# Four-layer graph network on one core: three of ScalarE's instructions in another place of its order

## Time and profile before

| | us |
|---|---|
| median of 3 runs | 5209.99 (5206.79 to 5223.11) |
| the profiled execution, its own time | 5213.31 |
| its span in the profile | 5211.5 |

### The profile page before, as it was taken

One profiled execution on the slowest core, in us unless ns is written; L12 is line 12 of the kernel. 1 busy time (PEld: TensorE's weight loads), 2 busy tenths in 40 slices (PEclk: granted clock), 3 DMA queues, 4 the chain that ended last, 5 costly groups with the idle time before them and its releaser, 6 DMA issues. The chain is left out here.

```text
span 5211.5 us, 74853 instructions
## 1 busy us (share of the span) xinstructions
PE 4348.2 (83%) x20185; PEld 3268.9 (63%) x20185; DVE 4031.9 (77%) x13139; ACT 2978.4 (57%) x7633; POOL 3114.9 (60%) x2813
## 2 busy tenths in 40 slices
PE   3999999999948888857777799999766648978887
PEld 2888888888836666635556466666444327766555
DVE  5899999999968888668888388888767668965554
ACT  2999999999924444424444377777545534521111
POOL 3766666666356666356666355555266636647776
PEclk8999999999979999978888899999877769999998
DMA  4888888888744444258877466666467766644443
GB/s 134 297 313 312 309 311 309 309 309 308 291 145 135 132 136 139 87 163 268 271 260 255 153 182 186 183 184 191 144 211 243 243 199 193 209 147 135 147 155 125
DMA packets 652112, 1097.58 MB, mean 211 GB/s; under 512 B 85506, under 2 KB 472458, under 8 KB 651573
## 3 DMA queue, kind: packets, MB, share of 16 engines
q1 hardware_dynamic: 532418, 838.42, 47.3%
q0 software_dynamic: 119168, 253.97, 16.6%
q10 hardware_dynamic: 112, 0.40, 0.0%
HBM read 524.78 MB, written 575.95 MB: 211 GB/s over the span
## 5 line engine op out<-in xcount | busy, mean ns | idle before, releaser
L855 PE MATMUL mm<-w,tt 128*128 128x264 f32 x3136 | 733.3, 387 | 2.6 <-ACT tt L899 2.6
L1414 POOL DMA_INDIRECT got<-F,index x392 | 524.0, 1337 | 312.3 <-PE acc L1605 207.6
L855 PEld LDWEIGHTS mm<-w,tt 128*128 128x128 f32 x3136 | 582.9, 191 | 93.2 <-ACT tt L899 2.8
L1601 PE MATMUL acc<-got,sel 128*128 128x260 f32 (+1 forms) x1176 | 441.8, 463 | 155.6 <-DVE sel L1576 147.0
L1614 ACT ACTIVATE rows<-acc 128x260 f32<-128x260 f32 (+1 forms) x588 | 227.4, 387 | 574.9 <-PE acc L1605 574.8
L821 POOL DMA_INDIRECT place<-PLACE,place_ix x392 | 415.0, 1059 | 119.5 <-issue 119.5
L2760 DVE SCALAR_TENSOR_TENSOR agg<-mask,agg,acc 128x128 f32<-128x128 f32 x784 | 247.7, 343 | 256.6 <-PE acc L2747 143.0
L793 POOL DMA_INDIRECT xd<-in_x_dram,index x196 | 224.9, 1147 | 317.1 <-DMA XD<-xd 285.5
L855 PE MATMUL mm<-wl,tt 128*128 128x264 f32 x1568 | 413.5, 387 | 1.0 <-ACT tt L899 1.0
L1601 PEld LDWEIGHTS acc<-got,sel 128*128 128x128 f32 x1176 | 251.8, 229 | 225.4 <-DVE sel L1576 134.4
L1294 PE MATMUL kv<-wkv,ht 128*128 128x512 f32 x784 | 371.5, 596 | 0.1
(11 more groups left out here) (414 smaller groups left out, 12938.1 us busy)
## 6 DMA issues: line engine op xcount, KB each, us to landing
F<-f1o SPq DMA_DIRECT2D x97, 528.0 KB
F<-f2o SPq DMA_DIRECT2D x97, 528.0 KB, 3.2
HL<-ho SPq DMA_DIRECT2D x97, 528.0 KB
xin<-in_x_dram SPq DMA_DIRECT2D x97, 512.0 KB, 5.5
H<-h SPq DMA_DIRECT2D x97, 512.0 KB, 3.2
X<-x3o SPq DMA_DIRECT2D x97, 512.0 KB, 3.3
out_dram<-oo SPq DMA_DIRECT2D x97, 512.0 KB
drow<-DSTF SPq DMA_DIRECT2D x84, 448.0 KB
```

The costliest lines, as they stand in the source:

```text
L855: last = nc.tensor.matmul(mm[PAIR[stage, q]][:, r, 0:F2W], lhs[:, q, 2 * r + k, :], w[:, k, :], start=(k == 0), stop=(k == KB - 1))
L1414: nc.gpsimd.indirect_dma_start(out=buf[:, n % SLOTS, t, :], out_offset=None, in_=table, in_offset=bass.IndirectOffsetOnAxis(ap=index[:, n ...
L1601: nc.tensor.matmul(acc, self.sel[:, s, t, :], self.got[:, n % SLOTS, t, 0:w], start=True, stop=False)
```

## The change

Only ScalarE's order changes, in three passes. No instruction, wait, buffer or transfer is added or removed.

```diff
 (first attention pass)
                             if within(a) and t == 4:
                                 ph.exponents(act, a)
-                            if within(x) and t == 6:
+                            if within(x) and t == GS:
                                 hold(act, d["x"], x + 1, None)
                                 hold(act, d["g"], x, None)
                                 nc.scalar.activation(zm[:, :, :], o[:, x % SLOTS, :, :], ACT.Relu, scale=-1.0)\
 (second attention pass)
                                 nc.scalar.activation(qo[:, e % 2, t - 2, :], qm[:, :], ACT.Copy).then_inc(d["q"], 1)
-                        if within(a):
-                            ph.exponents(act, a)
+                            if within(a) and t == 6:
+                                ph.exponents(act, a)
                     every(4, group)
 (single-head pass)
                         a, b, x, c = n, n - 1, n - 2, n - 3
-                        if within(b):
-                            for t in range(GS):
+                        for t in range(GS):
+                            if within(b):
                                 ph.take_rows(act, b, t)
-                        if within(c):
-                            hold(act, d["unc"], c + 1, None)
-                            nc.scalar.activation(th[:, :], unc[:, :], ACT.Tanh).then_inc(d["tanh"], 1)
+                            if within(c) and t == 3:
+                                hold(act, d["unc"], c + 1, None)
+                                nc.scalar.activation(th[:, :], unc[:, :], ACT.Tanh).then_inc(d["tanh"], 1)
                         if within(a):
                             ph.exponents(act, a)
```

## The result

The changed kernel takes 5193.9 us (median of 6 runs, 5189.6 to 5199.1) against 5213.5 (median of 6) for the kernel before, measured beside it; ratio 0.9961, 95% interval [0.9948, 0.9974]. It is 0.4% faster. The forecast was 5144 and its range ended at 5188: the direction was right, the size was not.

The account below looks back on a forecast made before the run. No engine is always busy; the waits that close each pass's loop bound the kernel. 5213.3 + 48 - 56 - 58 = 5147 us, with the median 3.3 lower: forecast 5144, 8-in-10 range 5104 to 5188.

Parts of the forecast that it names:

- First pass, the chain: First attention pass: the Relu starts 1.22 us later and lengthens the loop by that; 33 us over 27 bodies.
- Rival D: First attention pass: the exponential wait is only apparent and the later place is free; 5096 us, chance 0.06.
- First pass, the price of the pause: First attention pass: slow matmuls behind a 3.5 us TensorE pause at `edges` cost 0.6 us a body, 15 us.
- Second pass: Second attention pass: `exponents` earlier removes nearly all of `crow`'s wait for `wt`; -56 us (-62 to -40), period 20.4.
- Single-head pass, the chains: Single-head pass: with the tanh 3.5 us earlier, ScalarE's own loop closes and L2592 waits for the squares; -58 us.
- forecast floor of 14.2: Single-head pass: shortest period, about 14.2 us a body, from VectorE's chain over the squares; GpSimd's issues take 13.6.
- the period shrinks ... afterwards 14.8: Single-head pass: period falls from 17.09 us by 1.97 of ScalarE idling, 0.1 of tanh and some 0.2, to 14.8.
- rival A: Clock does not suffer: first pass pays 33 us alone, single-head pass gains 70, second 59; 5114 us, chance 0.17.
- rival B: Second and single-head gains half eaten by the next wait (`put`; GpSimd or the load of `he`); 5201 us, chance 0.11.
- Rival C: First attention pass: TensorE's clock stays low from `edges` to step 7's product in most bodies; up to 5345 us, chance 0.04.

## Why the prediction was wrong

- **First pass, the chain: right.** The Relu's place costs 1.22 us a body; with filled pauses the period was 25.80 against 25.79 worked out. Rival D (the later place is free) fell.
- **First pass, the price of the pause: the term was mis-sized.** The prediction took 0.6 us a body for matmuls at the lower clock behind the new pause: 1.6 us in six bodies of ten, less 0.3. It was 1.62 in most bodies and 1.9 on average (27.71 less 25.81). The 1.6 of one slow stretch was met, in part by luck, since it was built on one pause of 3.5 us behind `edges` where there were three, and the wait for the `hot` vectors (1.81 us at L1895) was not in it. How many bodies pay was wrong. Two things came together: the stretch moved from a place where it cost 0.3 to 0.5 us to one where each 1.62 counts, and it went from 12 of 24 bodies to 20 of 24. The place alone, at the old count, would have made about 0.6 a body (half of 1.62 less 0.4), an estimate from these rows; the rest is the count. The Trainium skill was weighed there ("TensorE: Matmul & The Clock Gate", "Why this matters for your kernels") with the reading that each body pays. Nearly each one did, but behind three pauses of 1.00, 1.81 and 1.34 us and not behind the one of 3.5 us for which the reading was made.
- **Second pass: right**, -54.9 against -56, period 20.35 against 20.4. VectorE bounds it.
- **Single-head pass, the chains: right.** ScalarE's own sequence closes the loop and L2592 waits; with filled pauses the period was 14.37, near the forecast floor of 14.2.
- **Single-head pass, "the period shrinks ... afterwards 14.8": the failed step.** It has no term for TensorE's clock: the old bodies' mix of fast and slow sums was carried over unchanged, and rival A even let it improve "since the pauses get shorter". The pause ahead of `turned` did get shorter (4.87 us became 2.10 and 0.99 in the bodies read), but a new one of up to 2.8 us opened inside the sums, ahead of L1605 of the second. The seven `take_rows` took 9.72 us against 8.73. That is 24 of the 28 us missing, and filling the pauses gave back 37.
- **The range.** The first pass's +72 lay inside its own bounds (33 to 100). The single-head pass's -30 lay outside its bounds (-47 to -70), because they had no clock term; so 5194 fell outside a range that ended at 5188. It is nearest to rival B's 5201, but B's mechanism did not come: the second pass kept its whole gain, and what the single-head pass lost went to slow sums and not to a load or to `put`. Rival C, which named the clock in the first pass, was priced only in its extreme.

Left open: which property of the pauses decides about the clock. The runs show that filling them ends the slow matmuls, and that these followed pauses of 1.0 to 1.8 us close together more often than a single pause of 2.84.

## What to carry to other kernels

Where TensorE works in bursts, add to each edit of another engine's order the question where TensorE's pauses will lie afterwards: with 1.20 us of slack behind it a slow stretch of 1.6 us cost 0.3 to 0.5, on the closing chain its whole length. An edit that takes a wait away from one engine can open one on TensorE, as the first copy behind the Exp or behind the squares did here. Here both passes that missed their forecast missed it by this term, so give it to every pass in which TensorE pauses. Before a result is put down to a wait, fill the pause with small matmuls into a free bank: it shows within one run whether the wait or the clock is paid for, if the fillers really lie in a pause. Here it brought 37 and 42 us in two passes, and nothing where part of the fillers had no pause to lie in.

## What the runs showed that was not expected

- Thirty-two bf16 matmuls of 256 columns a body (12, 8 and 12; twelve take 1.47 us) raised the granted clock of the single-head pass from 0.76 to 0.95, fillers included, without any change to the other instructions.
- The same fillers are worth 37 us with the tanh moved and nothing (-4 us) without: there the twelve ahead of the second sum stand on the closing chain with their own time.
- One pause of 2.84 us was followed by slow matmuls in 12 of 24 bodies; pauses of 1.00, 1.81 and 1.34 us close together were followed by them at once in 20 of 24.
- In the single-head pass the granted clock hardly moved (0.77 to 0.76), and yet the seven `take_rows` got 1.0 us longer: the slow sums had moved behind the first of them.
